# A bitwise split for VectorE's share of the exponentials, and a larger share

## The reference, cut to what matters

```python
def wl_step(acc, wl):
    cpm, iw = wl
    m = cpm[None, :, None, None]
    scores = jnp.einsum('bhqd,bhkd->bhqk', Q * m, K * m) * SCALE
    scores = scores * jnp.cos(KERR * scores * scores)
    attn = jax.nn.softmax(scores, axis=-1)
    out = jnp.einsum('bhqk,bhkd->bhqd', attn, V)
    return (acc + out * iw, None)
```

## Time and profile before

| | us |
|---|---|
| median of 3 executions | 3400.6 (3398.81 to 3402.12) |
| the profiled execution's own time | 3405.69 |
| its span in the trace | 3403.6 |
| ScalarE busy | 3316.2 (97%) |
| VectorE busy | 3240.6 (95%) |
| TensorE busy (matmuls) | 2650.6 (78%) |
| mean granted TensorE clock | 0.936 of full |

### The profile page before, as it was taken

One profiled execution on the slowest core, in us unless ns is written; L12 is line 12 of the kernel. 1 busy time (PEld: TensorE's weight loads), 2 busy tenths in 40 slices (PEclk: granted clock), 3 DMA queues, 4 the chain that ended last, 5 costly groups with the idle time before them and its releaser, 6 DMA issues.

```text
span 3403.6 us, 47606 instructions
## 1 busy us (share of the span) xinstructions
PE 2650.6 (78%) x20639; PEld 760.4 (22%) x20639; DVE 3240.6 (95%) x2747; ACT 3316.2 (97%) x611; POOL 229.2 (7%) x321
## 2 busy tenths in 40 slices
PE   7777877777777777778778788888877778788876
PEld 2212222222222222222222222222222222222224
DVE  7999999999999999999999999999999999999997
ACT  7999999999999999999999999999999999999992
POOL 0000000000000000000001111101111101111100
PEclk8999899999999999998999999899999999988888
DMA  1000000000000000000000000000000000000001
GB/s 49 1 1 1 1 1 1 1 1 1 1 1 1 1 1 1 1 15 1 1 1 3 4 3 4 2 1 4 2 4 2 4 1 2 4 3 16 2 17 31
DMA packets 21400, 16.05 MB, mean 5 GB/s; under 512 B 4865, under 2 KB 19602, under 8 KB 20946
## 3 DMA queue, kind: packets, MB, share of 16 engines
q1 hardware_dynamic: 19922, 12.28, 1.2%
q10 hardware_dynamic: 1152, 0.53, 0.1%
q0 software_dynamic: 128, 0.26, 0.0%
HBM read 7.70 MB, written 5.37 MB: 4 GB/s over the span
## 4 chain that ended last, share of the span: by engine, by line
ACT 59%; issue 32%; ACTq 4%; DVE 2%; PE 2%; DMA 0%; POOL 0%; DVEq 0%
ACT probs L694 56%; ACTq L684 4%; ACT probs L691 3%; PE psum L1392 1%; ACTq L688 0%; DVE s_t L921 0%; DVE probs L973 0%; DVE m_pad L909 0%; DMA iw<-nterference_weights_dram 0%; PE psum L948 0%; DVE probs L1003 0%; PE psum L1063 0%; PE psum L943 0%; PE psum L1106 0%; PE psum L933 0%
## 5 line engine op out<-in xcount | busy, mean ns | idle before, releaser
L694 ACT ACTIVATE probs<-s_t 128x8192 f32<-128x8192 f32 x447 | 3099.8, 7054 | 2.8 <-PE psum L1392 2.8
L1392 PE MATMUL psum<-probs,v_pad 128*27 128x512 f32 x15136 | 1909.2, 646 | 638.0 <-ACT probs L694 605.5
L1392 PEld LDWEIGHTS psum<-probs,v_pad 128*27 128x27 f32 x15136 | 462.1, 113 | 1996.9 <-issue 1022.1
L765 DVE SCALAR_TENSOR_TENSOR x_y<-s_t,c_last,x_2k 128x2048 f32<-128x2048 f32 (+1 forms) x160 | 369.6, 2310 | 2.3
L777 DVE SCALAR_TENSOR_TENSOR x_p<-x_p,x_y 128x2048 f32<-128x2048 f32 (+1 forms) x160 | 358.3, 2239 | 4.5
L785 DVE SCALAR_TENSOR_TENSOR x_p<-x_p,x_2k 128x2048 f32<-128x2048 f32 (+1 forms) x160 | 357.7, 2236 | 3.9
L781 DVE SCALAR_TENSOR_TENSOR x_p<-x_p 128x2048 f32<-128x2048 f32 (+1 forms) x160 | 357.3, 2233 | 2.4
L773 DVE SCALAR_TENSOR_TENSOR x_p<-x_y 128x2048 f32<-128x2048 f32 (+1 forms) x160 | 356.8, 2230 | 0.0
L921 DVE COPY s_t<-psum 128x2048 f32<-128x2048 f32 x128 | 292.2, 2284 | 9.4 <-PE psum L884 9.0
L909 DVE TENSOR_REDUCE m_pad<-psum 128x4 f32<-128x2048 f32 x128 | 292.4, 2286 | 5.8 <-PE psum L844 4.6
L762 DVE TENSOR_SCALAR x_2k<-s_t,c_last 128x2048 int16<-128x2048 f32 (+1 forms) x160 | 201.2, 1257 | 4.9 <-issue 1.0
(11 more groups left out here) (245 smaller groups left out, 1083.9 us busy)
## 6 DMA issues: line engine op xcount, KB each, us to landing
s_t<-in_L_attn_x_dram SPq DMA_DIRECT2D x4, 256.0 KB, 7.3
x_next_dram<-x_p SPq DMA_DIRECT2D x1, 1024.0 KB, 4.0
x_group<-x_next_dram SPq DMA_DIRECT2D x1, 1024.0 KB, 4.8
loop_memory<-in_L_attn_x_dram SPq DMA_DIRECT2D x8, 128.0 KB, 2.3
x_dram<-loop_memory SPq DMA_DIRECT2D x8, 128.0 KB, 1.8
out_dram<-loop_memory SPq DMA_DIRECT2D x8, 128.0 KB, 1.8
x_dram<-probs SPq DMA_DIRECT2D x2, 512.0 KB, 4.8
out_dram<-probs SPq DMA_DIRECT2D x2, 512.0 KB, 3.6
```

Of the source, the lines that this page charges most:

```text
L694: nc.scalar.activation(probs[:, (p + w) % 2, :], s_t[:, p, :], ACT.Exp, scale=scales[(p + w) % 2]).then_inc(s["exp_done"], 1)
L765: nc.vector.scalar_tensor_tensor(out=y, in0=scores, scalar=scale, in1=at, op0=ALU.mult, op1=ALU.subtract) \
L1392: last = nc.tensor.matmul(products_of(u, wg)[L * b:L * b + SLOTS * A, :], v_pad[:, p, b * T + kt, c0:c0 + SLOTS * A], probs[:, (p + w) % 2 ...
```

## The change

Two things change in the attention's pieces, and the tables follow.

**The split.** Operation 0 now scales by 2^23 more and rounds to a 32-bit integer, whose low 23 bits are the fraction and whose upper bits the power of two. Operation 1 takes the fraction with `and` and sets the exponent of 1.0 with `or`: one 32-bit input instead of two float inputs. Operation 2 makes the power of two with `xor` and `and` on 32 bits, in the place of an add and multiply on 16 bits. The polynomial's constants differ; its four operations stay.

**The share.** SHARED_B goes from (0, 1) to (3, 4), now counted in the third key tile: piece 4 is always the whole last key tile of channel 14 (2048 columns), and units 0 to 15 get a piece 5, the last 512 columns of the third key tile. ScalarE's step 14 shrinks from 6144 to 5632 columns in units 0 to 15 and from 6656 to 6144 in units 16 to 31. TensorE has as many matmuls as before; some of L1392 are now in pieces.

**The tables.** In units 0 to 15, piece operations and products have new steps; units 16 to 31 keep the five-piece tables.

```diff
-SHARED_B = (0, 1)
-ACT_LAST = [T * X_COLS - (NB - b) * S for b in SHARED_B]
-PIECES = T + 1
+SHARED_B = (3, 4)
+ACT_LAST = [(T - 1) * X_COLS - (NB - b) * S for b in SHARED_B]
+def pieces_of(u):
+    return T + 1 + (SHARED_B[u // H] < NB)
+def piece_no(u, n):
+    return sum(pieces_of(v) for v in range(u)) + n
...
-LOWEST_Y = -126.0
+FRACTION = 2 ** 23
+LOWEST_Y = -126.0 * FRACTION
+FRACTION_BITS, ONE_BITS = FRACTION - 1, 0x3f800000
+EXPONENT_TOP, EXPONENT_BITS = 0x40000000, 0x7f800000
...
-PIECE_STEPS = {0: (0, 3), 1: (3, 5), 2: (5, 6), 3: (6, 8), 4: (8, 10), 5: (10, 12), 6: (12, 15), 7: (15, 18), 8: (18, 19),
+FIVE_STEPS = {0: (0, 3), 1: (3, 5), 2: (5, 6), 3: (6, 8), 4: (8, 10), 5: (10, 12), 6: (12, 15), 7: (15, 18), 8: (18, 19),
                9: (19, 21), 10: (21, 22), 11: (22, 24), 12: (24, 27), 13: (27, 31), 14: (31, 35)}
-PRODUCT_STEPS = {6: 0, 8: 1, 11: 2, WA: 3, WA + 1: 4}
+SIX_STEPS = {0: (0, 4), 1: (4, 6), 2: (6, 7), 3: (7, 9), 4: (9, 11), 5: (11, 13), 6: (13, 16), 7: (16, 19), 8: (19, 21),
+               9: (21, 23), 10: (23, 25), 11: (25, 27), 12: (27, 31), 13: (31, 34), 14: (34, 42)}
+PIECE_STEPS = tuple(SIX_STEPS if b < NB else FIVE_STEPS for b in SHARED_B)
+FIVE_PRODUCTS = {6: 0, 8: 1, 11: 2, WA: 3, WA + 1: 4}
+SIX_PRODUCTS = {6: 0, 8: 1, 10: 2, 13: 3, 14: 4, WA: 5}
+PRODUCT_STEPS = tuple(SIX_PRODUCTS if b < NB else FIVE_PRODUCTS for b in SHARED_B)
...
-        x_2k = sb("x_2k", [P, X_COLS], BF16)
-        x_n = x_2k[:].bitcast(I16)
+        x_i = sb("x_i", [P, X_COLS], I32)
...
             if op == 1:
                 dve.wait_ge(s["piece_chain"], base + 1)
-                nc.vector.scalar_tensor_tensor(out=y, in0=scores, scalar=scale, in1=at, op0=ALU.mult, op1=ALU.subtract) \
+                nc.vector.tensor_scalar(y.bitcast(I32), at, FRACTION_BITS, ONE_BITS, ALU.bitwise_and, ALU.bitwise_or) \
                     .then_inc(s["piece_chain"], 1)
             if op == 2:
                 dve.wait_ge(s["piece_chain"], base + 2)
-                nc.vector.tensor_scalar(at, at, 127.0, 128.0, ALU.add, ALU.mult)
+                nc.vector.tensor_scalar(at, at, EXPONENT_TOP, EXPONENT_BITS, ALU.bitwise_xor, ALU.bitwise_and)
...
-                            for b in range(SHARED_B[g] if w == WA - 1 and kt == T - 1 else NB):
+                            for b in range(NB if w < WA - 1 or kt < T - 2 else SHARED_B[g] if kt == T - 2 else 0):
```

More of the change, by code:

```diff
@@ L73, in steps_of @@
 def steps_of(u, usual, last):
-    return last if u == UNITS - 1 else usual
+    return last if u == UNITS - 1 else usual[u // H]
 def due(u, w, usual, last):
@@ L752, in piece_dve @@
         def piece_dve(dve, n, op, u, p, h):
-            piece, base = u * PIECES + n, (u * PIECES + n) * PIECE_LINKS
-            w, start, cols = (W - 1, n * X_COLS, X_COLS) if n < T else (WA - 1, ACT_LAST[u // H], T * X_COLS - ACT_LAST[u // H])
+            piece, base = piece_no(u, n), piece_no(u, n) * PIECE_LINKS
+            w, start, cols = ((W - 1, n * X_COLS, X_COLS) if n < T else (WA - 1, (T - 1) * X_COLS, X_COLS) if n == T
+                              else (WA - 1, ACT_LAST[u // H], (T - 1) * X_COLS - ACT_LAST[u // H]))
             scores = s_t[:, p, start:start + cols]
             scale = c2_last[:, w - (WA - 1), h:h + 1]
-            at, y, t = x_n[:, 0:cols], x_y[:, 0:cols], x_p[:, piece % 2, 0:cols]
+            at, y, t = x_i[:, 0:cols], x_y[:, 0:cols], x_p[:, piece % 2, 0:cols]
             if op == 0:
@@ L784, in piece_dve @@
                 dve.wait_ge(s["piece_chain"], base + 5)
-                nc.vector.scalar_tensor_tensor(out=t, in0=t, scalar=EXP2_D, in1=x_2k[:, 0:cols], op0=ALU.add, op1=ALU.mult) \
+                nc.vector.scalar_tensor_tensor(out=t, in0=t, scalar=EXP2_D, in1=at.bitcast(F32), op0=ALU.add, op1=ALU.mult) \
                     .then_inc(s["piece_ready"], 1)
         def piece_pe(pe, n, u):
-            pe.wait_ge(s["piece_ready"], u * PIECES + (n + 2))
+            pe.wait_ge(s["piece_ready"], piece_no(u, n) + 2)
             if n == 0:
                 pe.wait_ge(s["o_copied"], max(u * NWG + 1, 2))
-            wg, kt = (NWG - 1, n) if n < T else (LAST_OF[WA - 1], T - 1)
+            wg, kt = (NWG - 1, n) if n < T else (LAST_OF[WA - 1], T - 1 if n == T else T - 2)
             c0 = VPAD if n < T else VPAD - A * SLOT_OF[WA - 1]
-            for b in range(NB) if n < T else range(SHARED_B[u // H], NB):
-                at = b * S if n < T else (b - SHARED_B[u // H]) * S
+            first, latest = SHARED_B[u // H] if n > T else 0, pieces_of(u) - 1
+            for b in range(first, NB):
+                at = (b - first) * S
                 last = nc.tensor.matmul(products_of(u, wg)[L * b:L * b + SLOTS * A, :],
-                                        v_pad[:, u % 2, b * T + kt, c0:c0 + SLOTS * A],
-                                        x_p[:, (u * PIECES + n) % 2, at:at + S], start=(n == 0), stop=(n == T - 1 or (n == T and u < UNITS - 1)))
+                                        v_pad[:, u % 2, b * T + kt, c0:c0 + SLOTS * A], x_p[:, piece_no(u, n) % 2, at:at + S],
+                                        start=(n == 0), stop=(n == T - 1 or (n >= T and n == latest and u < UNITS - 1)))
             last.then_inc(s["piece_used"], 1)
@@ L1395, in _ @@
                                     start=(kt == 0 and w in FIRST_OF),
-                                    stop=(w in LAST_OF and kt == (T - 2 if u == UNITS - 1 and w == WA - 1 and b >= SHARED_B[g] else T - 1)))
+                                    stop=(w in LAST_OF and kt == T - 1) or (w == WA - 1 and kt == T - 2 and products_end_here(u)))
                         last.then_inc(s["pv_done"], 1)
@@ L1494, in _ @@
                     dve.wait_ge(s["c2_step"], 7)
-                    nc.vector.tensor_scalar(c2_last[:], c2[:, WA - 1:W, :], LOG2_E, None, ALU.mult).then_inc(s["piece_used"], 1)
+                    nc.vector.tensor_scalar(c2_last[:], c2[:, WA - 1:W, :], LOG2_E * FRACTION, None, ALU.mult).then_inc(s["piece_used"], 1)
                 prep_dve(dve, step, 0, 0, first=True)
```

18 lines of the change are left out of this document (10 added, 8 removed).

## The result

| | before | changed |
|---|---|---|
| median, us (lowest to highest) of 4 runs each, side by side | 3401.4 (3398.8 to 3403.8) | 3499.7 (3499.1 to 3501.6) |
| profiled execution: own time, span | 3405.7, 3403.6 | 3499.5, 3497.7 |
| mean granted TensorE clock | 0.936 | 0.909 |

The ratio is 1.0287 [1.0274, 1.0299]: 2.9% slower, 98.3 us by the medians. The spans differ by 94.1 us; the profiled execution of before lay some 4 us above its median, which is the difference. The forecast was 3476 us with a range that ended at 3492: the direction came out, and in units 0 to 15 the mechanism; the size did not. The time lies 7.7 us above the range, by two errors of some 10 us each: one in units 0 to 15, and one in the second half, where a gain was forecast and a loss came.

The account below looks back on a forecast made before the run. ScalarE was taken to set the pace, VectorE almost as long. A loop of 69.2 + 4.4 + 28.1 + 5.6 = 107.3 us per unit gave +79, units 16 to 31 -4: 3400.6 + 75 = 3476 us, range 3438 to 3492.

Parts of the forecast that it names:

- the loop: Units 0 to 15: path through ScalarE, VectorE and TensorE, closed by piece 4's early product; 107.3 us per unit against 102.35.
- ScalarE, steps 1 to 10: ScalarE's part of each unit in units 0 to 15: ten steps at 6.92 us, 69.2 us.
- start of step 11 to weigh(2): From ScalarE's step 11 to VectorE's weigh(2), which waits for TensorE's transposes: 4.4 us, however fast VectorE is.
- weigh(2) to the end of piece 4: VectorE's back-to-back operations from weigh(2) to piece 4's last operation, summed from start-to-start times: 28.1 us.
- TensorE, end of piece 4 to ScalarE's step 1: Piece 4's four matmuls and step 14's eleven, mostly at the slow clock: 5.6 us, bounds 3.4 and 6.1.
- units 16 to 31: -4, bounds -7 and +4: Second half of the units: same order, no loop; ScalarE's and VectorE's work let eight pairs shrink, -4 us in all.
- Rival A: Pace stays ScalarE's or VectorE's, whose work sums are even, and the change pays: 3387 to 3397 us; chance 0.06.
- Rival C: The loop closes but TensorE's clock is full at once: fifteen matmuls in 3.4 us, 3441 us; inside the range, no separate chance.

## Why the prediction was wrong in its size

The four terms of the loop, for unit 8 and as the mean of units 0 to 15:

| term | predicted | unit 8 | mean |
|---|---|---|---|
| ScalarE, steps 1 to 10 | 69.2 | 10 * 6.925 = 69.25 | 69.25 |
| start of step 11 to weigh(2) | 4.4 | 980.68 - 975.42 = 5.26 | 4.97 |
| weigh(2) to the end of piece 4 | 28.1 | 1008.54 - 980.68 = 27.86 | 27.87 |
| TensorE, end of piece 4 to ScalarE's step 1 | 5.6 | 1015.03 - 1008.54 = 6.49 | 6.0 |
| sum | 107.3 | 108.86 | 108.08 |

(Step 11 of unit 8 began at 906.17 + 10 * 6.925 = 975.42.)

- **The loop, its place and VectorE's part: right.** Nineteen VectorE operations were summed from rows of before, with two whose kind no row had, and came within 0.25 us. The bitwise passes were put at 1.3 and 1.2 us start to start and took 1.26 and 1.14 (L783 at 995.45, L787 at 996.71, L791 at 997.85), at lengths of 1.247 and 1.224. The rows still show what a wait for one's own engine costs: L795 and L799, where the second waits for the first, start 2.33 us apart, L799 and the reciprocal behind it, which does not wait for it, 2.21. The sentence weighed there from the Trainium skill, "VectorE: DVE Perf Modes", section "The DRAIN you can't avoid", that a semaphore after each operation costs nothing extra, would have put this term 0.7 below the sum; it came 0.23 below, and the rows above differ by 0.12 us, so here the measurement goes against it.
- **Failed: "TensorE 5.6, bounds 3.4 and 6.1".** The measured mean is 6.0, and the worst kind of unit has 6.49, above the bound. That the clock would be low was right. What was mis-sized is the count: I took 15/16 of the mean of two slow rows, 5.33 and 6.55, but these fifteen matmuls take as long as sixteen. At the full level, in the run with eight unused ones, they ran from 1313.55 to 1314.43 + 2.75 = 1317.18, 3.63 us, where sixteen take 3.64. Nor did I count the 0.06 us from VectorE's end to TensorE's start (1008.54 to 1008.60) and as much again to ScalarE. Sixteen and 0.12 give 5.94 + 0.12 = 6.06, bounds 3.76 and 6.67, and all units of the changed kernel, 5.23 to 6.50, lie within. Worth 0.4 a unit. The idleness ahead was longer than I had it, 8.03 us in unit 8 for 5.7, in part because step 13 ran at the full level (3.64 us, 5.33 before); the four matmuls behind it took 1.93 us against 1.06.
- **Failed: "weigh(2) begins 4.4 us after step 11".** It is a lower bound, which I used as the value. In two units of three the slow clock reaches one place more: TensorE's step 9 at 968.66 took 5.33 us (3.64 in the third), so the scores behind it come late, VectorE waits for them (1.92 us at 975.13), one step ahead of weigh(2), and from there works up to it without a gap. So weigh(2) still had its gap in one unit of three only, 0.79 us. The offset rotates through 4.41, 5.25 and 5.25, ScalarE's wait through 5.0, 5.9 and 6.95. Worth 0.57 a unit. The trace of before had the sign of it: in its units 3 and 14 weigh(2) begins 5.06 and 5.09 us after step 11, behind such a wait for scores, and in unit 5 6.11; I read unit 8 alone. Why the clock at step 9 alternates between units, no run here settles.
- Less 0.23 us in the VectorE term, and with 0.05 for the rounded step of ScalarE, these make the 0.78 a unit. Fifteen units at +5.73 are +85.9 us, and from step 14 of unit 15 to that of unit 16 it took 106.9 us where 103.64 stood, +3.3: 89.2 where 79 was forecast.
- **Failed: "units 16 to 31: -4, bounds -7 and +4".** They cost +5.9. I said "same order as before, so no such loop" and counted only VectorE's and ScalarE's work. But a path was there: from the statistics over piece 4's four long operations to L1022, and from it over TensorE to ScalarE's step 3. The larger piece makes it 2.1 us longer. And it was long already by GpSimd, which I left out since its busy time is 7%: its two-column operations take their length from VectorE's, and VectorE waits 1.7 us for the last of them, before as after. Taking back the 512 columns ends the loss, and so does shortening that wait by 1.1 us.
- Rival A was refuted by the order, but not its throughput half: with the products later and TensorE kept busy around step 13 the engines do keep up. Rival C's clock, forced by the eight unused matmuls, gave 3466, not 3441: its TensorE term was nearly right (3.75 against 3.4), the offset of weigh(2) was not (4.96 in most units), and the second half was wrong as above (103.34 us a unit).

## What to carry to other kernels

Before moving a step to the front of an in-order engine, ask which engine made its input last and when, and what stands behind it that another engine waits for: a product that was harmless one step later closed a loop through three engines and cost 89 us, while the sums of work stayed even. When pricing such a wait, count also the work behind it at the slow level of TensorE's clock, and use an offset read from an undisturbed unit as a bound, not as a value. And lengthen an operation only after following the path that stands behind it in its own engine's order, with the engine whose small operations it holds up, even one that is 7% busy.
